# A banded-attention tower: the band as a 0/1 factor behind the exponential instead of masks and a correction product

## The reference, cut to what matters

```python
scores = jnp.einsum('bhcqd,bhckd->bhcqk', qc, kb) / sqrt(16)      # chunks of 64 queries, 192 keys
allowed = mb & pos_ok & band_ok                                    # |q - k| <= 64, key exists, not padding
scores = jnp.where(allowed, scores, -1000000000.0)
probs = jax.nn.softmax(scores, axis=-1)
out = jnp.einsum('bhcqk,bhckd->bhcqd', probs, vb)
```

## Time and profile before

| | us |
|---|---|
| median of 3 runs | 7051.08 (7049.91 to 7069.48) |
| profiled execution | 7050.01 |
| its span, first to last instruction | 7048.2 |
| busy: TensorE | 6042.4 |
| busy: VectorE | 4250.6 |
| busy: ScalarE | 2239.1 |
| busy: GpSimd | 1101.6 |
| mean granted TensorE clock | 0.939 of 2.4 GHz |

### The profile page before, as it was taken

The page is one execution under the profiler, slowest core; times in us unless marked ns, Lnnn a source line. Parts: engine busy times, 40 slices in busy tenths (PEclk is TensorE's granted clock), DMA queues, the critical chain, the costliest instruction groups (busy, mean ns, idle before and its releaser), DMA issues. The chain is left out here.

```text
span 7048.2 us, 128877 instructions
## 1 busy us (share of the span) xinstructions
PE 6042.4 (86%) x46786; PEld 4744.2 (67%) x46786; DVE 4250.6 (60%) x11172; ACT 2239.1 (32%) x4196; POOL 1101.6 (16%) x1089
## 2 busy tenths in 40 slices
PE   1999999999999999999999999978888883289999
PEld 0777777777777777777777777756666662266766
DVE  6666666666666666666666666666666664722222
ACT  0333333333333333334333333323333330011111
POOL 5011111111111111111111111111111110234333
PEclk9999999999999999999999999989999986699999
DMA  6322223323232322222332232332222320033322
GB/s 119 62 60 60 60 61 65 70 61 66 58 64 60 75 61 60 60 60 60 67 70 61 62 65 60 65 69 56 62 64 63 64 56 10 1 84 73 88 69 55
DMA packets 1204450, 441.09 MB, mean 63 GB/s; under 512 B 1050338, under 2 KB 1191044, under 8 KB 1204324
## 3 DMA queue, kind: packets, MB, share of 16 engines
q1 hardware_dynamic: 1176676, 402.69, 26.7%
q0 software_dynamic: 27648, 36.72, 3.4%
HBM read 124.23 MB, written 60.26 MB: 26 GB/s over the span
## 5 line engine op out<-in xcount | busy, mean ns | idle before, releaser
L673 ACT ACTIVATE pT<-bank 128x384 f32<-128x384 f32 x1920 | 907.9, 490 | 872.8 <-PE bank L511 872.8
L843 DVE TENSOR_REDUCE mx<-bank 128x2 f32<-128x384 f32 x1548 | 802.2, 554 | 322.0 <-PE bank L483 285.1
L582 PE MATMUL bank<-hT,w 96*128 96x256 f32 x3072 | 848.0, 442 | 85.9 <-ACT hT L688 85.9
L582 PEld LDWEIGHTS bank<-hT,w 96*128 96x128 f32 x3072 | 678.6, 224 | 236.2 <-ACT hT L688 118.2
L509 PE MATMUL bank<-maskb,eyeb 128*128 128x384 bf16 x1920 | 635.1, 331 | 78.6 <-ACT pT L673 73.3
L481 PE MATMUL bank<-maskb,eyeb 128*128 128x384 bf16 x1932 | 634.5, 328 | 39.9 <-DMA qkT<-stack 20.7
L483 PE MATMUL bank<-qkT 128*128 128x192 bf16 (+2 forms) x3864 | 636.5, 247 | 0.0
L511 PE MATMUL bank<-qkT 128*128 128x192 bf16 (+2 forms) x3840 | 630.9, 246 | 0.0
L993 DVE TENSOR_TENSOR hout<-bank,resid 128x384 f32<-128x384 f32 x128 | 71.3, 557 | 769.4 <-PE bank L594 769.4
L594 PE MATMUL bank<-w,pT 128*128 128x192 f32 x3072 | 520.4, 326 | 0.0
L1022 POOL TENSOR_TENSOR rstd<-ve,half 128x2 f32<-128x2 f32 x160 | 127.7, 798 | 2486.6 <-DVE ve L749 2486.6
(11 more groups left out here) (197 smaller groups left out, 10230.5 us busy)
## 6 DMA issues: line engine op xcount, KB each, us to landing
hcur<-hbuf SPq DMA_DIRECT2D x165, 192.0 KB, 2.4
hbuf<-hout SPq DMA_DIRECT2D x128, 192.0 KB, 2.0
amb<-am_d SPq DMA_DIRECT2D x131, 128.0 KB, 2.9
exp_wg<-in_ewg SPq DMA_DIRECT2D x16, 768.0 KB
exp_wu<-in_ewu SPq DMA_DIRECT2D x16, 768.0 KB
exp_wd<-in_ewd SPq DMA_DIRECT2D x16, 576.0 KB
xs<-xr SPq DMA_DIRECT2D x32, 272.0 KB, 2.2
hbuf<-emb_z SPq DMA_DIRECT2D x17, 384.0 KB
```

The lines of the kernel that those rows point to most:

```text
L582: last = nc.tensor.matmul(bank[s][f // 2][:, (f % 2) * S:(f % 2 + 1) * S], w1[:, c, f * P:(f + 1) * P], hT[s][:, c, :], start=(c == 0), st ...
L673: ph.inc(nc.scalar.activation(pT[s][:, h % NPT, :], bank[s][h % 2][:, 0:SCOLS], ACT.Exp, scale=SCALE), "p", s)
L843: last = nc.vector.tensor_reduce(mx[s][:, :, h], src[:, 0:SCOLS].rearrange("p (t k) -> p t k", t=T), AX, ALU.max)
```

## The change

The second pass no longer adds a mask. Its exponentials come out for all keys, and VectorE multiplies four heads at a time by a 0/1 tile (`dve_keep`), with a minimum of 3e38 ahead of the factor so that an overflow times 0 is 0. In token layers the tile is `keys`, built per sequence by GpSimd as the band plus, where a whole window is padding, the rest of the window; so the unkept product, `wam` and its addition go. A padded query or key row is multiplied by `live`. The attention products wait for the multiplied tile (`kept`) and stand behind loop steps 8, 12 and 15. Maxima are taken for two heads in one instruction, over four banks in turn instead of three. The biases of queries, keys and values become a 97th row of the weights against a row of ones; ScalarE takes the values, and the high part of queries and keys, out of PSUM, and VectorE the low part.

```diff
-PLAN = Plan(prod=(6, 10, 13), rows=3, vadd=3)
+PLAN = Plan(prod=(8, 12, 15), keep=(1, 3, 5))
         def pe_scores1(...)
-            if h >= 3:
-                ph.wait(pe, "mx", s, F.it, h - 2)
-            dst = bank[s][h % 3]
+            if h == 3:
+                ph.wait(pe, "y" if causal else "r2", s, F.it, 0)
+            if h >= 4 and h % 2 == 0:
+                ph.wait(pe, "mx", s, F.it, h // 2 - 1)
+            dst = bank[s][h % 4]
         def pe_scores2(...)
-            nc.tensor.matmul(dst[:, 0:SCOLS], eyeb[:], maskb[:, masks + 1, :], start=True, stop=False)
         def pe_products(...)
-            ph.wait(pe, "p", s, K.it, 4 * g + 4)
+            ph.wait(pe, "kept", s, K.it, g + 1)
-            if K and not causal:
-                pe_unkept(ph, pe, K)
+        def act_v(ph, act, V, K, causal):
+            ph.wait(act, "v_ps", s, V.it)
+            if K:
+                ph.wait(act, "otT_ps", K.s, K.it)
+            ph.inc(nc.scalar.copy(vaug[s][:, :, :, 0:DH],
+                                  bank[1 - s][0][:, 0:2 * D].rearrange(...)), "v", s)
+        def act_top(ph, act, G):
+            for t in range(T):
+                ph.wait(act, "qk_ps", s, G.it, t + 1)
+                ph.inc(nc.scalar.activation(stack[s][:, t]..., bank[s][1 + t][:, 0:2 * D]..., ACT.Copy,
+                                            scale=live[...]), "qh", s)
+        def dve_rest(ph, dve, G):
+            for t in range(T):
+                ph.wait(dve, "qh", s, G.it, t + 1)
+                ph.inc(nc.vector.scalar_tensor_tensor(rem[s][:, t]..., bank[s][1 + t][:, 0:2 * D]...,
+                    live[...], stack[s][:, t]..., ALU.mult, ALU.subtract), "qk", s)
+        def dve_keep(ph, dve, K, g, mask):
+            ph.wait(dve, "p", s, K.it, 4 * g + 4)
+            p = pT[s][:, (4 * g) % NPT:(4 * g) % NPT + 4, :]
+            ph.inc(nc.vector.scalar_tensor_tensor(p, p, 3.0e38, mask.unsqueeze(1).to_broadcast([P, 4, SCOLS]),
+                                                  ALU.min, ALU.mult), "kept", s)
         def vector_half(...)
+            for p in range(NH // 2):
+                if F:
+                    dve_row_max(ph, dve, F, p, qcols)
+                    if causal and p == 3:
+                        input_norm_begin(ph, dve, F._replace(it=F.it + 1))
+                    if causal and p == 4:
+                        input_norm_end(ph, dve, F._replace(it=F.it + 1))
+                if K and p in PLAN.keep:
+                    if p == PLAN.keep[0] and not causal:
+                        ph.wait(dve, "keys", K.s, K.it)
+                    dve_keep(ph, dve, K, PLAN.keep.index(p), seen[:, 2, :] if causal else keys[K.s][:])
-                if not causal:
-                    dve_add_unkept(ph, dve, bc, K)
-                dve_v(ph, dve, V)
-            if G:
-                dve_qk(ph, dve, G)
+            if G and not causal:
+                dve_rest(ph, dve, G)
         def pool_half(...)
+            if F and not causal:
+                for t, (c0, f0, w) in enumerate(BAND_COLS):
+                    ph.inc(nc.gpsimd.tensor_tensor(keys[s][:, c0:c0 + w], seen[:, 1, c0:c0 + w],
+                                                   amb[s][:, f0:f0 + w], ALU.mult), "kw", s)
+                ph.wait(pool, "kw", s, F.it)
+                ph.inc(nc.gpsimd.tensor_tensor(keys[s][:], keys[s][:], seen[:, 0, :], ALU.add), "keys", s)
```

## The result

The changed kernel takes 8849.1 us in the median of four runs (8831.9 to 8858.1); the kernel before takes 7050.5 (four runs, 7048.5 to 7069.5). The ratio is 1.254, with a 95% interval of 1.251 to 1.257. The profiled execution took 8844.9 us.

A forecast was written before the change was run, and what follows sets the result against it. TensorE was taken as the bound. Token half 5.15 + 0.5 + 3.1 = 8.75 us, x 128 = 1120; causal half 11.6, x 31 = 360; 7050 + 1480 = 8530 us, range for 8 in 10 7930 to 8930.

The forecast's parts named there:

- VectorE's product: Second pass, three in each half: multiplying four heads (1536 elements) by the 0/1 tile takes 1.76 us.
- The in-order walk: Token half: TensorE waits 2.3, 2.5 and 3.1 us for VectorE's products; output transposes start at 18.90 us, before 13.15.
- The 5.15 us a token half: Token half at full clock: output transposes 5.75 us later, less 0.61 for the dropped addition of the unkept product.
- GpSimd's tile: Token half, end of first norm: building the key tile slows two VectorE instructions by 0 to 0.7 us, taken as 0.5.
- The clock: Each half: TensorE's clock falls after the new waits for VectorE, costing 0 to 5.3 us, taken as 3.1.
- Causal half: Causal layer: 7.9 us for the walk, 0.6 for rotary steps beside the norm, 3.1 for the clock: 11.6 us.
- the main case: Whole kernel: 8530 us with chance 0.58, its own range 8300 to 8800.
- The saving on TensorE: Token half: 12 dropped masks (2.0 us) and the unkept product (1.30) save 3.3 us if nothing else becomes late.
- the clock holds: Rival: TensorE's clock does not fall; 5.65 us a token half, 8.5 a causal one, 8037 us; chance 0.22.
- third rival: Clock falls at every first wait and VectorE's product is dear; 12.15 us a token half, 9070 us; chance 0.08.
- The cheap product: Rival: VectorE's product runs at two elements per cycle, 0.8 us less each; 7814 us; chance 0.08.
- the not-slower case: Rival: VectorE's product ends before TensorE reaches the attention products, needing under about 0.2 us; about 7070 us; chance 0.04.

The follow-up runs named there:

- e_fillall: The changed kernel with spare matmuls in all long waits: 20 before each wait for VectorE's product, 14 and 10 before the up projection; 7948.5 us, ratio 1.133.
- b_fill: The kernel before with 14 and 10 spare matmuls in its two waits ahead of the up projection; 6786.7 us, ratio 0.968.
- e_seqmask6: The changed kernel without VectorE's product; TensorE adds the second-pass mask from a GpSimd tile, attention products at steps 6, 10 and 13; 7144.6 us, ratio 1.013.
- e_seqearly: e_seqmask6 with GpSimd's operations on the sequence's tile moved directly behind its work on the residual; 6997.2 us, ratio 0.992.
- e_late: e_seqearly with GpSimd's rotary steps in the causal layer waiting until VectorE has written the normed rows; 6861.5 us, ratio 0.978.
- e_noprod: The changed kernel without VectorE's 0/1 product, attention products waiting for the exponentials, band left out of the second pass; 6820.6 us, ratio 0.972.
- e_halfprod: The changed kernel with VectorE's product over two of each four heads, the others unmasked; 8123.8 us, ratio 1.158.

## Why the prediction was right, and where it was short

**VectorE's product:** 1.76 us predicted, 1.747 measured.

**The in-order walk:** waits of 2.3, 2.5 and 3.1 us, output transposes at 18.90. With the clock held (e_fillall) they are at 18.95, spare work and wait together are 2.2, 2.5 and 3.1 us, and the three groups of products at 7.28, 12.64 and 17.52, where 7.24, 12.58 and 17.45 were predicted: it is not the sum alone that came out. In the changed kernel the waits are 2.12, 2.08 and 2.71 (shorter, as TensorE is later at half clock) and the place is 23.14. The 5.15 us a token half nearly stand: e_fillall less b_fill is 39.79 - 33.62 = 6.17 us, of which 0.65 is GpSimd's, so 5.5.

**GpSimd's tile:** 0.5 predicted, 0.65 measured as a wait (1.59 to 0.94, e_seqmask6 to e_seqearly).

**The clock:** this is the term that was mis-sized. 10.37 - 6.17 = 4.2 us a token half, where 3.1 was taken, between bounds of 0 and 5.3. Two parts of it can be told apart. The prediction had no clock term on the wait for the norm, though it foresaw that this wait would grow: the up projection takes 911 us of busy time for 848, and 697 in both e_fillall and b_fill, so 0.5 of the 4.2 us lies there. The other 3.7 lie behind the waits for VectorE. That not every group falls was right; what was too low is the price of a half in which all fall. In the half shown first, the output transposes come 23.14 - 18.95 = 4.2 us later than with the clock held, and they and the transposes of the maxima take 0.6 and 1.2 us more: 6.0 us for the 5.3. The single products were priced too high (0.65 us more each, not 0.8). The score groups were priced too low: behind the first product eleven rows follow each other at 0.32 us where it was 0.165, and behind the second six, together some 2.5 us for 1.5. So were the transposes behind the third: 0.45, 0.6 and 1.2 us more, 2.2 for 1.4. Shorter waits give a part of that back. Over the token stretch one matmul of the attention products takes 383 ns for 277.

**Causal half:** 11.6 predicted, 13.87 measured, 2.3 x 31 = 70 us. The collision with the rotary steps was foreseen and priced at 0.6 us, which was too low; e_late shows 1.44 directly and 3.1 with what the clock adds. With the long waits filled the half is 45.30 - 34.17 = 11.1 us above b_fill's, so queue and collision make up most of it. The walk came out nearly: in the half of e_fillall that begins at 5635.49 the output transposes start at 22.06 us and the groups of products at 8.20, 14.69 and 20.63, where 21.7 was predicted for the transposes and 8.1, 14.6 and 20.2 for the ends of VectorE's products. The clock of e_fillall was not held up in full in the causal layer (the shared up projection takes 435 ns a matmul, in b_fill 397), so I leave the split at that.

**The sum:** 10.37 us a token half for 8.75, of which the clock is 1.1, the queue 0.37 and GpSimd 0.15. In the whole stage 1316 us for 1120, so 196 are missing there, 70 in the causal layer, 22 in the setup (under 2 us predicted), 18 between the stages and 8 behind: 314 of the 315. The time lies inside the range for 8 in 10 (7930 to 8930) and outside the one that was given for the main case (8300 to 8800): nearly all the terms missed to the same side, and the upper bound left 80 us.

**The saving on TensorE:** "3.3 us if nothing else becomes late" was not seen by itself in the changed kernel. e_noprod shows 1.9 of it in the token half, less what GpSimd's tile costs there.

**Rivals:** "the clock holds" would have been 8037 us, 987 above before. No run has that state: e_fillall nearly holds the clock but fills the gaps of the kernel before too, so it has to be laid beside b_fill, and there the change costs 6.17 us a token half and 11.1 a causal one, for 5.65 and 8.5. The clock did not hold, and the time lies 319 us above the forecast and 220 below the third rival's 9070. The cheap product and the not-slower case fell with 1.747 us.

## What to carry to other kernels

Work moved from a busy engine to an idle one can cost little in busy time and much in order: ask whose next input stands behind it, and walk both queues. Read how long the matmuls behind a wait take as well as the wait; here the waits that recur in each half were paid a second time at 1.2 GHz, and spare matmuls in them gave that back. Look at many iterations, as the clock differs from one to the next. An instruction moved off an engine releases what waited for it earlier, here GpSimd, which then slowed the very VectorE instructions on the path.

## What the runs showed of the hardware that was not expected

TensorE's clock: 24 spare matmuls a half, 1.7 us of work without use, made the kernel before 3.2% faster. The level behind a wait does not follow from the wait's length alone. In e_halfprod the second group of products kept the full clock in all 124 halves behind waits of 1.52 us in the mean, the first in only 71 behind shorter ones of 1.27. Behind 2.1 us the first group was at half clock throughout in 91 of 123 halves of the changed kernel, and the third in 1 of 124 of e_halfprod (in the half shown the output transposes behind it took 1.54 us for 0.87). Waits of 0.94 and 0.67 us with 0.64 us of transposes between them were followed by an up projection of 7.1 us in 54 of 107 halves of e_seqearly, of more than 8 in 13 and of 5.45 in 40. What decides between these the runs leave open.

VectorE beside GpSimd: four TENSOR_SCALARs on float32 took 2.62 us for 1.20, a factor of 2.2; reductions from PSUM were not slowed.
